# Adaptive-LayerNorm block on one core: the residual additions of the third token tile move from GpSimd to the vector engine

## The reference, cut to what matters

```
mod = silu(c) @ wmod                         # sa, ca, ga, sb, cb, gb per batch
ga, gb: sign kept, size at least 0.25
attn = (w1.T @ w2.T) * sparse_mask           # 1024 x 1024, mask is a band
h = layernorm(x) * (1 + ca) + sa
x = x + ga * gelu(h @ attn + b2)             # first half
h = layernorm(x) * (1 + cb) + sb
gate, up = split((h @ U1) @ V1 + b1)
x = x + gb * (((silu(gate) * up) @ U2) @ V2 + b2f)   # second half
```

## Time and profile before

| | us |
|---|---|
| median of 3 runs | 1197.95 (1196.84 to 1201.61) |
| profiled execution | 1196.55 |
| its span, first to last instruction | 1194.7 |

### The profile page before, as it was taken

The page is one execution under the profiler, slowest core; times in us unless marked ns, Lnnn a source line. Parts: engine busy times, 40 slices in busy tenths (PEclk is TensorE's granted clock), DMA queues, the critical chain, the costliest instruction groups (busy, mean ns, idle before and its releaser), DMA issues.

```text
span 1194.7 us, 15376 instructions
## 1 busy us (share of the span) xinstructions
PE 1143.3 (96%) x5882; PEld 943.0 (79%) x5882; DVE 587.0 (49%) x937; ACT 491.4 (41%) x787; POOL 390.5 (33%) x339
## 2 busy tenths in 40 slices
PE   5588999999999999999999999999999999999998
PEld 5357898887778788888888888888888888888886
DVE  1557687786665334434444344443543434344343
ACT  0037577676777543224224323323322432332241
POOL 1007899891112657313031130211303113021110
PEclk9899999999999999999999999999999999999999
DMA  9984998857553642421040150122113015013001
GB/s 358 360 311 149 339 343 302 310 190 271 212 211 129 199 143 79 163 85 71 28 149 3 69 176 1 71 90 87 71 50 127 23 48 176 1 71 122 20 1 70
DMA packets 57197, 169.61 MB, mean 142 GB/s; under 512 B 6176, under 2 KB 10784, under 8 KB 55072
## 3 DMA queue, kind: packets, MB, share of 16 engines
q1 hardware_dynamic: 57120, 168.57, 39.4%
HBM read 126.51 MB, written 42.04 MB: 141 GB/s over the span
## 4 chain that ended last, share of the span: by engine, by line
PE 84%; DMA 4%; DVE 4%; ACT 3%; issue 2%; SPq 1%; POOL 1%; DVEq 0%; ACTq 0%
PE bank L537 23%; PE bank L538 23%; PE bank L539 23%; PE bank L702 6%; PE bank L597 4%; PE bank L576 2%; DMA mask_a<-in_mask 2%; ACT nrm L957 2%; PE bank L688 1%; DMA pt_dram<-pt_st 1%; DVE h_lo L1316 1%; DMA wm_sb<-in_wmod 1%; DVE bn L1183 1%; PE bank L877 1%; SPq L377 1%
## 5 line engine op out<-in xcount | busy, mean ns | idle before, releaser
L1121 ACT ACTIVATE act<-bank,b_sb 128x512 f32<-128x512 f32 (+1 forms) x176 | 121.3, 690 | 497.3 <-PE bank L539 481.4
L1448 DVE SCALAR_TENSOR_TENSOR act<-bank,b_sb,act 128x512 f32<-128x512 f32 (+1 forms) x176 | 131.9, 750 | 376.2 <-PE bank L539 352.8
L537 PE MATMUL bank<-pt,v_hi 128*128 128x512 f32 x688 | 268.8, 391 | 1.3 <-DVE act L1448 1.3
L538 PE MATMUL bank<-pt,v_hi 128*128 128x512 f32 x688 | 267.7, 389 | 0.0
L539 PE MATMUL bank<-pt,v_lo 128*128 128x512 f32 x688 | 267.7, 389 | 0.0
L1599 POOL TENSOR_TENSOR x2t<-gbb_bc,x2t 128x512 f32<-128x512 f32 x64 | 85.4, 1357 | 250.8 <-DMA x2t<-x_dram 250.8
L1458 DVE TENSOR_TENSOR act_lo<-act,act_hi 128x512 fp32r<-128x512 f32 (+1 forms) x176 | 160.5, 912 | 0.9
L537 PEld LDWEIGHTS bank<-pt,v_hi 128*128 128x128 f32 x688 | 129.1, 188 | 31.7 <-DVE act L1448 4.3
L539 PEld LDWEIGHTS bank<-pt,v_lo 128*128 128x128 f32 x688 | 129.2, 188 | 27.1
L538 PEld LDWEIGHTS bank<-pt,v_hi 128*128 128x128 f32 x688 | 129.2, 188 | 26.1
L537 PE MATMUL bank<-act_hi,u_hi 128*128 128x512 f32 x336 | 130.9, 390 | 0.7 <-DVE act_lo L1458 0.6
(11 more groups left out here) (134 smaller groups left out, 1670.0 us busy)
## 6 DMA issues: line engine op xcount, KB each, us to landing
wm_sb<-in_wmod SPq DMA_DIRECT2D x9, 2048.0 KB, 10.3
xs<-in_x SPq DMA_DIRECT2D x32, 512.0 KB, 5.6
x_dram<-xs SPq DMA_DIRECT2D x32, 512.0 KB, 5.1
xs<-x_dram SPq DMA_DIRECT2D x32, 512.0 KB, 5.5
x2t<-x_dram SPq DMA_DIRECT2D x32, 512.0 KB, 4.1
out<-x2t SPq DMA_DIRECT2D x32, 512.0 KB, 4.9
pt_dram<-pt_st SPq DMA_DIRECT2D x8, 1024.0 KB, 7.5
pt<-pt_dram SPq DMA_DIRECT2D x8, 1024.0 KB, 5.7
```

The source lines that it names most:

```text
L537: nc.tensor.matmul(acc, s_hi, m_hi, start=start, stop=False)
L538: nc.tensor.matmul(acc, s_hi, m_lo, start=False, stop=False)
L1121: nc.scalar.activation(act[0:w, j % 2, :], bank[0:w, j % 2, :], ACT.Silu, bias=b1_sb[0:w, i, 0:1]).then_inc(silu_done, 1)
L1448: nc.vector.scalar_tensor_tensor(act[0:w, j % 2, :], up, b1_sb[0:w, i, 1:2], act[0:w, j % 2, :], ALU.add, ALU.mult).then_inc(act_done, 1)
```

## The change

`on_vector` now also names token tile 2. So in batches 1 to 7 DVE adds units 2, 3, 6, 7 and POOL 0, 1, 4, 5; in batch 0 DVE adds 1, 2, 3, 5, 6, 7 and POOL 0 and 4. That is two additions more on DVE in each batch, 16 in all. The new calls are put into DVE's order by hand, and `add(b, 3)` moves one `lo` later. All waits on `added` follow by themselves: ACT's gelu, SP's stores. No other engine's order is edited.

```diff
         def on_vector(b, u):
-            return u % TT == TT - 1 or b == 0 and u % TT == 1
+            return u % TT >= 2 or b == 0 and u % TT == 1
@@ before the loop
             lo(1, 0)
             add(0, 1)
-            for k in range(1, 4):
-                lo(1, k)
+            lo(1, 1)
+            add(0, 2)
+            lo(1, 2)
+            lo(1, 3)
@@ in the loop over b
                 lo(b, 4)
+                if b > 1:
+                    add(b - 1, 6)
                 lo(b, 5)
                 if b > 1:
                     add(b - 1, 7)
...
                 lo(b, 7)
                 if b == 1:
+                    add(0, 6)
                     add(0, 7)
                     stats2(0, 0)
...
                 lo(b + 1, 1)
-                add(b, 3)
+                add(b, 2)
                 stats(t, 2)
                 lo(b + 1, 2)
+                add(b, 3)
                 stats(t, 3)
                 lo(b + 1, 3)
@@ after the loop
                 lo(t, 4)
                 if b == 0:
                     beta2_rows()
+                    add(NB - 1, 6)
                     add(NB - 1, 7)
```

## The result

The changed kernel takes 1210.89 us (median of 4, 1208.02 to 1213.66) against 1197.39 (4, 1196.48 to 1201.61). The ratio is 1.0106, 95% interval 1.0071 to 1.014: slower by 13.5 us by the medians and by 12.7 by the ratio, where the sum of the forecast was 9.2 (9.6 by 1207 less 1197.39). The interval of the ratio stands for 8.5 to 16.8 us and so holds the forecast, so how much the forecast fell short is read from the trace and the experiments, not from these eight runs. The profiled execution is the slowest of the four, span 1211.5 us; it began the attention stage 2.4 us late, which is scatter of the start (its first `turn(1,0)` stands at 102.86, at 100.45 before, and at 99.45 to 103.06 in executions whose code up to there is the same).

The account below looks back on a forecast made before the run. The prediction took the attention stage as PE-bound with DVE's queue close behind; terms 2.4 + 3.6 + 2.3 + 0.9 = 9.2 us on the median 1197.95 gave 1207 us, slower, with a range of 1202 to 1213.

Parts of the forecast that it names:

- rival (3): Attention stage: x loads and stores crowd and come late in three iterations, 1210 us, up to 1213; chance 0.10.
- What bounds the kernel: Attention stage: PE-bound with DVE's queue close behind; nobody waits for POOL's additions although POOL is 91% busy.
- Slack of 0.44 us, price 1.23, loss 0.79 per iteration: Iterations 2 to 4: one more addition in DVE's chain to `lo(b+1,4)`; 2.4 us in all, bounds 0.7 and 3.2.
- `add(b-1,6)` free behind the `lo`: Between `lo(b,4)` and `lo(b,5)`: hidden in DVE's idle time, cost 0; without that cover 0.7 to 1.3 us each.
- Iterations 1, 5, 6 at 1.2 each: PE already waits for `lo(b+1,4)` there, so the whole addition is paid: 3.6 us, bounds 2.0 and 4.5.
- Batch 0 to 1: Crossing between batches: `add(0,2)` delays `gelu(0,6)` and `add(0,6)` delays `stats2(0,0)`; 2.3 us, bounds 0.7 to 3.2.
- Start of the second half: Batch 7's last stores wait for `add(7,6)` on DVE, so the reload comes later: 0.9 us, bounds 0 and 2.
- iteration 7: DVE waits there and PE has 24 more products between the units: cost 0, bounds 0 and 1.2 us.

Follow-up runs that it names:

- e5: Kernel before, with POOL's additions of token tile 2 cut to 2 of 512 columns and nothing moved to DVE: 1199.53 us, ratio 1.0004.
- e6: Kernel before, with `stats2(b,0)` moved from ahead of `lo(b+1,4)` to behind it in iterations 1 to 6: 1195.57 us, ratio 0.9985.
- e12: e6 with batch 0's `add(0,1)` put ahead of `lo(1,0)` and `add(0,3)` ahead of `lo(1,2)`: 1194.77 us, ratio 0.9973 to the kernel before.
- e2: Changed kernel with batch 0 put back as before, so only batches 1 to 7 are changed: 1207.55 us, ratio 1.0079 to the kernel before.
- e3: Kernel before, with only unit 2 of batches 1 to 7 moved to DVE: 1204.63 us, ratio 1.0054.
- e9: e3 with DVE's addition of unit 2 cut to 2 of 512 columns: 1204.13 us, ratio 1.0044 to the kernel before.
- e10: e3 with POOL's addition of unit 5 in batches 1 to 7 cut to 2 of 512 columns: 1201.66 us, ratio 1.0023 to the kernel before.
- e4: Kernel before, with only unit 6 of batches 1 to 7 moved to DVE, behind `lo(b,4)`: 1200.70 us, ratio 1.001.
- e1: Kernel before, with only batch 0's two additions (units 2 and 6) moved to DVE: 1202.83 us, ratio 1.0044.
- e11: e2 with e6's later `stats2`, batch 0 as before: 1198.71 us, ratio 0.9999 to the kernel before.
- e7: Changed kernel with `stats2(b,0)` moved behind `lo(b+1,4)`: 1205.07 us, ratio 1.0058 to the kernel before.
- e8: e1 with `add(0,2)` directly behind `add(0,1)`, ahead of `lo(1,1)`: 1200.93 us, ratio 1.0023 to the kernel before.

## Why the prediction was right

It was right in sign, mechanism and range (1202 to 1213), and some 4 us short in size by the trace (9.2 against 13.4). The upper end doesn't follow from its own working: rival (3)'s 1210 with the upper bound of batch 0's term is 1211, not 1213. That the measured 1210.89 lies under both is no merit of the sum.

- *What bounds the kernel*: right. e5 shows POOL's 91% to be worth nothing, e6 and e12 that DVE's order is.
- *Slack of 0.44 us, price 1.23, loss 0.79 per iteration*: right; 0.82 in after (2.46 for three), 0.81 in e2 and e3. PE's wait shows 0.56 and not the 0.8 forecast, because the wait view starts at the modelled end of the product before. That POOL's running instruction and not the work makes most of the price is shown by e9 and e10.
- *`add(b-1,6)` free behind the `lo`*: right (e4).
- *Iterations 1, 5, 6 at 1.2 each*: right for 5 and 6 where the clock holds (1.12 in e2, 1.13 in after's 6). For iteration 1 it was 0.76 in e2; in after it is hidden under what batch 0 brings (1.89 us, and 1.84 in e1 without it).
- *Batch 0 to 1, "0.7 to 3.2", taken 2.3*: the step that failed in size; 4.4 by e1, 4.0 in its trace (2.20 and 1.84). `add(0,2)` took 1.76 us, over the bound of 1.50 that I took from 18 additions; the rule of the Trainium skill (SBUF — State Buffer, "Who interferes with whom") had allowed 1.95. `add(0,6)` and `add(0,7)`, back to back, let a POOL instruction in between and took 2.89 us together, where `add(0,7)` alone had taken 1.11 (POOL's addition is issued at 121.01, behind its product of 119.64, which ended at 120.93, and takes 1.62 us). And `stats2(0,0)` so began 20.25 us after `turn(1,0)` and not 16.08. What `add(0,3)` and `add(0,5)` gave back (0.68 us each, 1.45 and 1.50 before) did not lie on the path: DVE waited for ACT behind them. DVE's rows of after, then POOL's:

```profile
108.30 1.76 DVE L1211 TENSOR_TENSOR xs<-g,xs 128x512 f32<-128x512 f32 x1
...
120.29 2.89 DVE L1211 TENSOR_TENSOR xs<-g,xs 128x512 f32<-128x512 f32 x2
123.11 2.46 DVE L1199 BATCH_NORM_STATS2 bn<-xs 128x6 f32<-128x512 f32 x4
...
133.52 1.29 DVE L1183 BATCH_NORM_STATS2 bn<-xs 128x6 f32<-128x512 f32 x2 [2.98 <-DMA xs<-in_x]
```

```profile
119.64 1.29 POOL L1534 TENSOR_TENSOR g<-g,ga_bc 128x512 f32<-128x512 f32 x1 [3.48 <-ACT g L983]
121.01 1.62 POOL L1537 TENSOR_TENSOR xs<-g,xs 128x512 f32<-128x512 f32 x1
```

- *Start of the second half, 0.9*: the time fits by luck. Of after's 1.02 us, 0.9 is the clock and 0.1 is left for the term; PE's wait at `turn(9,3)` was 0.65 in e4 and 1.41 in e11, but also 1.13 in e3, where unit 6 stays on POOL. The term is not shown. Ahead of it after has 1.5 us more of "issue" at `turn(8,4)` (2.65 against 1.15), where the forecast put 0 on iteration 7; it was 1.19 to 2.11 in e1 to e4 and 1.89 in e5, with nothing moved to DVE, so it is not shown to be the change's, and its cause stays open.
- *The clock*: no term of the sum; 3.2 us in the trace of after. What the forecast lacks there, 4.2 us, is 1.0 in the two stretches after batch 0 (0.7 of it the clock), 1.5 in iteration 5 (the clock) and 1.6 ahead of `turn(8,4)`. Of this only the crossing's part is shown to come back with the change, by e1 and e7.
- *Rival (3), loads late*: not in after's iterations 2 to 4. Single iterations of 22.9 to 23.0 us with DVE late for x occur in the traces of e1, e5, e7 and e8, in e5 with nothing moved to DVE, so they are scatter that this schedule is exposed to.

## What to carry to other kernels

Before work goes from an engine that looks full to one that looks half idle, ask who waits for either: here the 91% engine had no one behind it, and the 78% engine had 0.44 us of slack ahead of PE's next operand. Find that slack from an iteration of the same trace in which the chain happens to be longer. An engine's queue has free places (behind the awaited instruction, in the idle time ahead of one) and dear ones; moving `stats2` behind the awaited `lo` (e6) was worth more than any of the divisions of the additions that were tried.

## What the runs showed of the hardware that was not expected

An addition of 2 columns on DVE took about as long as one of 512 that meets no large POOL instruction (0.77 against 0.68 us), as it sat out POOL's instruction. Two waiting additions in a row take turns with POOL: 2.89 us for the pair. PE's lower clock stood behind waits of 1.7 to 3.9 us, but not behind each of them: behind a wait of 1.90 us at `turn(1,4)` the kernel before kept 1.00, while e3 and e6, alike up to there, had 0.54 and 0.55. The two rows are before's and e3's; what decides between them stays open.

```profile
108.73:112.00 3.27, 3.27 (x27) 2.94 (x27) 2.63 (x4) 1.86 (x3) 3.19 (x4) 1.00 0.41 167
```

```profile
108.47:112.00 3.53, 3.53 (x18) 3.53 (x19) 2.95 (x4) 1.86 (x3) 3.45 (x4) 0.54 0.39 160
```
